# Scores and values of an attention as 64x64 tiles, causal values by key quarters, value banks copied by two engines

## The chip, the cores and the metric

The kernel runs on one core of a Trainium2 chip. Its engines are PE (TensorE, matmuls), ACT (ScalarE), DVE (VectorE), POOL (GpSimd) and SP (SyncE, which issues DMAs). The metric is the device time of one execution in microseconds, as the median of several runs.

## The reference

The input x is (8, 256, 128), in float32. Four blocks are added to it in turn, each on a layer norm of x:

```python
# 1: attention a, 16 heads of 64, over 256 tokens, with a relative bias
scores = einsum('bhid,bhjd->bhij', q, k) * 64**-0.5 + bias
out = einsum('bhij,bhjd->bhid', softmax(scores), v) ... @ w_out.T
# 2: a mixture of 8 experts: router, LN, W1 (128x512), relu, W2 (512x128), times the gate
# 3: attention b, keys and values from a latent (128), causal
att = where(causal, q @ k * 64**-0.5, -inf); y = softmax(att) @ v ... @ w_out
# 4: the same mixture of experts again
```

The function says T = 32 for attention b in its setup, but it takes its length from x, which is 256. In attention a channels of w_qkv are laid out as (d, c, h): the head is the fastest index.

## The kernel before, in words

Each engine has a program of its own, written by hand as a list of steps s. Semaphores tie them: `x.wait_ge(sem, n)` waits, `.then_inc(sem, 1)` signals. The first stage (st = 0) is attention a and its experts, the second (st = 1, causal) attention b and its experts. A stage of attention has 8 batches of 8 units, NU = 64. A unit u is a pair of heads over 256 queries and 256 keys.

One unit goes through these steps. `QK(u)` projects queries and keys of the unit into the bank PT_ (L572), six matmuls in fp32r of high and low parts, and ACT copies them to `qk` (`T`, L918): head 0 lies on partitions 0 to 63, head 1 on 64 to 127. DVE adds the bias or the mask, takes the minimum and writes the scores to `ring` (L1252). ACT takes the exponential in place and the row sum (`expo`, L954), DVE the reciprocal (L1263), POOL weighs the row (L362). `TR(u)` transposes the weighted scores on PE into the banks PP, head 0 in ps4 and head 1 in ps5 (L615, L630); ACT copies the first to `pt` (L932) and DVE the second (L1272). `PV(u)` multiplies by the values: 128 rows (keys) by 64 columns (one head), into one bank PO = ps6, a unit on a half of it (L634). After two units `keep` evicts PO: ACT rounds the bank to `oh` (L908), DVE takes the rest to `ol` (L1222). After eight units `out(b)` projects (L658).

Value matmuls (`values`, L556) make four banks of 128 tokens by 512 channels in a batch, and ACT copies each to `a_v` (L924); spare banks go around among ps1, ps2, ps3 and ps7, which S uses too (`spare`, `claim`).

The order on PE in a step is: QK(s), value matmuls, small pieces, TR(s-4), out. In odd steps S(s-1), S(s), PV(s-5), PV(s-4) follow (L826 to L831). So there is one run of S and PV for each two steps, which is called a step pair. ACT in an even step: keep, T, values, TR, exponentials. DVE in an even step: keep, pieces of the layer norms, TR; in an odd one: TR, S, S.

## Time and profile before

| what | value |
|---|---|
| median of 3 runs | 664.43 us (663.93 to 664.85) |
| span of the profiled execution | 662.1 us |
| median less span | 2.3 us |
| PE, PEld busy | 644.1, 543.7 us |
| DVE, ACT, POOL busy | 475.5, 533.7, 354.5 us |
| granted TensorE clock | 1.00 |

The median is that of the runs; the span is from the first to the last instruction of the one profiled execution. Busy is the time in which at least one instruction of the engine runs; matmuls overlap, so PE is busy also where its pace could be higher. PEld is the loading of weights, which runs beside the matmuls.

### The profile page before, as it was taken

The page shows a single profiled execution, that of the slowest core. Times are in us where ns is not written, and L with a number is a line of the kernel's source. Part 1 is how long each engine was busy: PE and PEld are TensorE (multiplying, and loading weights), DVE is VectorE, ACT ScalarE, POOL GpSimd, SP SyncE. Part 2 cuts the span into 40 slices and gives each one's busy share as a digit, 9 for nine tenths or more (in the row PEclk, how much of TensorE's full clock was granted, in tenths as well). Part 3 has the DMA queues.
Part 4 walks back from the last instruction along what each step waited for, and adds up shares of the span by engine and source line. Part 5 has one row for each costly group of instructions (what it writes and reads, how often), then busy time and mean ns, then how long its engine had stood idle before and what let it go on. Part 6 is the DMA issues. An engine that isn't in the chain of part 4 may idle for free. (4 is left out here: it accounts for less than half of the span.)

```text
span 662.1 us, 17840 instructions
## 1 busy us (share of the span) xinstructions
PE 644.1 (97%) x5406; PEld 543.7 (82%) x5406; DVE 475.5 (72%) x2147; ACT 533.7 (81%) x1776; POOL 354.5 (54%) x669
## 2 busy tenths in 40 slices
PE   5999999999999999999999999999999999999997
PEld 4778887888888788879997788888888888888997
DVE  4866767777786767988755667687768777898834
ACT  3997888889787978785765989898989898986664
POOL 4654545575546644732116545464757575572746
PEclk9999999999999999999999999999999999999999
DMA  9999999999992000035421000000000000003140
GB/s 262 292 296 290 286 230 313 298 272 280 289 286 87 25 1 2 33 98 163 131 65 41 21 1 1 3 1 9 17 15 9 14 25 2 2 34 101 52 132 16
DMA packets 86844, 74.48 MB, mean 112 GB/s; under 512 B 8001, under 2 KB 83399, under 8 KB 86496
## 3 DMA queue, kind: packets, MB, share of 16 engines
q1 hardware_dynamic: 82288, 66.24, 36.5%
q0 software_dynamic: 2848, 6.33, 3.0%
q10 hardware_dynamic: 1616, 0.79, 0.5%
q8 instruction: 45, 0.74, 0.5%
q14 instruction: 47, 0.39, 0.2%
HBM read 19.93 MB, written 54.00 MB: 112 GB/s over the span
## 5 line engine op out<-in xcount | busy, mean ns | idle before, releaser
L362 POOL TENSOR_SCALAR ring<-ring,rs 128x256 f32<-128x256 f32 (+1 forms) x500 | 218.7, 456 | 204.9 <-DVE rs L1263 204.0
L954 ACT ACTIVATE ring<-ring,mn 128x256 f32<-128x256 f32 (+1 forms) x512 | 243.2, 487 | 1.5 <-DVE mn L1252 1.5
L500 PE MATMUL ps<-ident,ring 128*128 128x128 f32 x896 | 120.8, 274 | 1.3 <-POOL ring L362 0.7
L611 PE MATMUL ps<-qk 64*128 64x256 f32 (+1 forms) x1024 | 115.2, 363 | 0.9 <-DVE mn L1252 0.7
L648 PE MATMUL ps<-pt,v 128*64 128x256 f32 (+1 forms) x1024 | 111.4, 359 | 0.2
L500 PEld LDWEIGHTS ps<-ident,ring 128*128 128x128 f32 x896 | 102.1, 143 | 7.6 <-POOL ring L362 2.1
L954 ACT ACTIVATION_READ_ACCUMULATOR ring<-ring,mn 128x1 f32 x512 | 103.6, 202 | 0.0
L648 PEld LDWEIGHTS ps<-pt,v 128*64 128x64 f32 x1024 | 65.5, 136 | 44.4 <-issue 13.3
L611 PEld LDWEIGHTS ps<-qk 64*128 64x128 f32 x1024 | 82.6, 186 | 18.8 <-issue 9.9
L922 ACT COPY qk<-ps 128x512 f32<-128x512 f32 x128 | 74.9, 585 | 23.6 <-PE ps L497 21.9
L1252 DVE CUSTOM_DVE_ANT_0 ring<-ps,cm 128x128 f32<-128x128 f32 (+1 forms) x256 | 73.8, 351 | 1.5 <-issue 1.2
L1281 DVE COPY pt<-ps 128x512 f32<-128x512 f32 x64 | 44.1, 690 | 35.6 <-PE ps L500 35.6
L495 PE MATMUL ps<-xth,wqkh 128*128 128x256 f32 x192 | 64.6, 336 | 0.0
L1003 ACT ACTIVATE f_ht<-ps,f_w 128x128 f32<-128x128 f32 x136 | 38.6, 378 | 21.7 <-PE ps L753 21.7
L1252 DVE CUSTOM_DVE_ANT_0 ring<-ps,T 128x256 f32<-128x256 f32 x136 | 55.5, 417 | 0.0
L497 PE MATMUL ps<-xtl,wqkh 128*128 128x256 f32 x192 | 53.8, 280 | 0.0
L496 PE MATMUL ps<-xth,wqkl 128*128 128x256 f32 x192 | 53.6, 279 | 0.0
L769 PE MATMUL ps<-w,f_ht 128*128 (+1 forms) x400 | 52.4, 277 | 0.4 <-ACT f_ht L1003 0.4
L876 ACT ACTIVATE oh<-ps 128x512 fp32r<-128x512 f32 x64 | 38.3, 598 | 16.7 <-PE ps L648 16.6
L495 PEld LDWEIGHTS ps<-xth,wqkh 128*128 128x128 f32 x192 | 36.0, 188 | 18.6 <-issue 17.4
L1252 DVE CUSTOM_DVE_ANT_1 ring<-ps,T 128x256 f32<-128x256 f32 x120 | 50.0, 417 | 0.2 <-PE ps L611 0.2
L769 PEld LDWEIGHTS ps<-w,f_ht 128*128 128x128 f32 x400 | 48.1, 192 | 1.7 <-issue 1.5
(212 smaller groups left out, 1334.4 us busy)
## 6 DMA issues: line engine op xcount, KB each, us to landing
xs_scratch<-f_ys SPq DMA_DIRECT2D x16, 2064.0 KB, 22.4
yr_scratch<-f_ys SPq DMA_DIRECT2D x8, 1024.0 KB, 10.8
f_xs<-xs_scratch SPq DMA_DIRECT2D x50, 129.0 KB, 2.4
w<-in_W SPq DMA_DIRECT2D x16, 256.0 KB, 6.0
xs_scratch<-f_ys SPq DMA_DIRECT2D x2, 1677.0 KB, 21.8
yr_scratch<-f_ys SPq DMA_DIRECT2D x25, 64.0 KB, 1.6
T<-in_bias SPq DMA_DIRECT2D x2, 512.0 KB, 8.1
T<-in_bias SPq DMA_DIRECT2D x1, 1024.0 KB, 11.0
```

Source lines behind the costliest of these rows:

```text
L362: i = pool.tensor_scalar(ring[:, hh, it, 0:w], ring[:, hh, it, 0:w], rs[:, q], 1.0, ALU.mult, ALU.mult)
L495: pe.matmul(out, ah, bh, start=first, stop=False)
L496: pe.matmul(out, al, bh, start=False, stop=False)
L497: return pe.matmul(out, ah, bl, start=False, stop=last)
L500: return pe.transpose(out, src, ident[:, :])
L611: i = pe.matmul(PS[u % 2][hh][:, 256 * it:256 * it + w], qk[rows, 128 * it:128 * it + 128], qk[rows, 256:256 + w], start=True, stop=True)
L648: i = pe.matmul(PO[64 * hh:64 * hh + 64, col + lo:col + 256], a_v[b % 2][:, jt, 128 * c + 64 * hh:128 * c + 64 * hh + 64], a_pt[(U0 + u) % ...
L769: i = pe.matmul(y_bank(n)[:, 0:128], f_ht[n % 3][:, 128 * f:128 * f + 128], w2[:, bass.ds(e * 4 + f, 1), :].rearrange("p a n -> p (a n)"), ...
L922: act.copy(a_qk[(U0 + u) % 2][:, :], PT_[:, :]).then_inc(a_t, 1)
L954: i = act.activation(ring[:, hh, it, 0:w], ring[:, hh, it, 0:w], ACT.Exp, bias=mn[:, q], scale=-1.0, accum_out=sm[:, q])
L1252: i = dve.tensor_tensor_reduce(ring[:, hh, it, 0:w], bank[:, 256 * it:256 * it + w], table(st, 2 * c + hh, it), 1.0, BIG, ALU.add, ALU.min ...
L1281: i = dve.tensor_copy(pt[:, 1, :], PP[1][:, :])
```

## The change

The ring holds a unit's weighted scores by 64 keys and head, `[it, quarter, head, 64]`, so that one 128x128 transpose gives 64 keys of head 0 on rows 0 to 63 and the same keys of head 1 on rows 64 to 127. S is made by four 64x64 tiles, PV by four 64x64 tiles for each quarter of the keys; PV is called for two units at once, and writes two banks, ps6 (head 0) and ps5 (head 1), which is also the bank of the second half of the transposes. In the causal stage quarter q takes queries from 64q on. Values lie head by row half, so that of each value bank ACT copies 64 partitions and DVE the other 64, to the other half. The order of the heads changes with it (`head_of`, `by_parity`), and the weights of attention b are loaded in ten DMAs with this order in place of two. The bank of the first expert tile's Y becomes ps4.

```diff
-    PO = ps[6]
+    PO = ps[6], ps[5]
-    a_ring = [sb(f"ring{i}", [128, 2, 2, 256], scope=base) for i in range(4)]
+    a_ring = [sb(f"ring{i}", [128, 2, 4, 2, 64], scope=base) for i in range(4)]
-    a_v = [sb("v0", [128, 2, 1024], scope=base)]
+    a_v = [sb("v0", [128, 4, 512], scope=base)]
...
+    def scores(ring, hh, it, w):
+        return ring[:, it, 0:w // 64, hh, :]
+    def by_64(a):
+        return a.rearrange("p (q d) -> p q d", d=64)
+    def head_of(u, hh):
+        return u // 2 * 4 + 2 * hh + u % 2
...
     # PE, S(u)
-                for hh in range(2):
-                    rows = slice(64 * hh, 64 * hh + 64)
-                    i = pe.matmul(PS[u % 2][hh][:, 256 * it:256 * it + w], qk[rows, 128 * it:128 * it + 128],
+                for half_, hh in ((0, 0), (1, 1), (1, 0), (0, 1)):
+                    rows, cols = slice(64 * hh, 64 * hh + 64), slice(64 * half_, 64 * half_ + 64)
+                    i = pe.matmul(PS[u % 2][hh][cols, 256 * it:256 * it + w],
+                                  qk[rows, 128 * it + 64 * half_:128 * it + 64 * half_ + 64],
                                   qk[rows, 256:256 + w], start=True, stop=True)
     # PE, TR(u)
-            for hh in range(2):
-                bank = PP[hh]
+            for jt in range(2):
                 if U0 + u:
-                    pe.wait_ge(v_pt1 if hh else a_pt0, U0 + u)
-                for jt in range(2):
+                    pe.wait_ge(v_pt1 if jt else a_pt0, U0 + u)
+                if U0 + u and jt and u % 2 == 0:
+                    pe.wait_ge(v_o, (U0 + u) // 2)
+                for q in (2 * jt, 2 * jt + 1):
                     for it in range(2):
                         if causal and jt > it:
                             continue
-                        i = tr(bank[:, 256 * jt + 128 * it:256 * jt + 128 * it + 128],
-                               ring[:, hh, it, 128 * jt:128 * jt + 128])
+                        i = tr(PP[jt][:, 256 * (q % 2) + 128 * it:256 * (q % 2) + 128 * it + 128],
+                               ring[:, it, q, :, :].rearrange("p h d -> p (h d)"))
     # PE, PV(u), now for u and u + 1
-            pe.wait_ge(a_pt0, U0 + u + 1)
-            pe.wait_ge(v_pt1, U0 + u + 1)
+            pe.wait_ge(a_pt0, U0 + u + 2)
+            pe.wait_ge(v_pt1, U0 + u + 2)
...
-            for jt in range(2):
-                lo = 128 if causal and jt == 1 else 0
-                for hh in range(2):
-                    i = pe.matmul(PO[64 * hh:64 * hh + 64, col + lo:col + 256],
-                                  a_v[b % 2][:, jt, 128 * c + 64 * hh:128 * c + 64 * hh + 64],
-                                  a_pt[(U0 + u) % 2][:, hh, 256 * jt + lo:256 * jt + 256], start=(jt == 0), stop=(jt == 1))
-            i.then_inc(t_pv, 1)
+            for q in range(4):
+                lo = 64 * q if causal else 0
+                for k, hh in ((0, 0), (1, 1), (0, 1), (1, 0)):
+                    rows = slice(64 * hh, 64 * hh + 64)
+                    i = pe.matmul(PO[hh][64 * k:64 * k + 64, lo:256],
+                                  a_v[b % 2][rows, q, 64 * (c + k):64 * (c + k) + 64],
+                                  a_pt[(U0 + u + k) % 2][rows, q // 2, 256 * (q % 2) + lo:256 * (q % 2) + 256],
+                                  start=(q == 0), stop=(q == 3))
+            i.then_inc(t_pv, 2)
...
     # ACT: keep, values, TR
-            act_high(a_oh[:, c:c + 2, :].rearrange("p c n -> p (c n)"), PO[:, :], a_o)
+            for hh, bank in enumerate(PO):
+                i = act.activation(a_oh[:, c + hh, :], bank[:, 0:256], ACT.Copy, scale=1.0)
+            i.then_inc(a_o, 1)
-            act.copy(a_v[b % 2][:, j, r], ps[bank_of[("v", st, b, n)]][:, :]).then_inc(a_vs, 1)
+            rows = slice(64 * half_, 64 * half_ + 64)
+            act.copy(a_v[b % 2][rows, 2 * j + half_, :], ps[bank_of[("v", st, b, n)]][rows, :]).then_inc(a_vs, 1)
-            if causal:
-                act.copy(pt[:, 0, 0:256], PP[0][:, 0:256])
-                i = act.copy(pt[:, 0, 384:512], PP[0][:, 384:512])
-            else:
-                i = act.copy(pt[:, 0, :], PP[0][:, :])
-            i.then_inc(a_pt0, 1)
+            act.copy(pt[:, 0, :], PP[0][:, :]).then_inc(a_pt0, 1)
     # DVE: values (new, in a step after keep and pre_b, pre_c), keep, TR
+            dve.tensor_copy(a_v[b % 2][64 * half_:64 * half_ + 64, 2 * j + 1 - half_, :],
+                            ps[bank_of[("v", st, b, n)]][64 - 64 * half_:128 - 64 * half_, :]).then_inc(v_vs, 1)
-            low(a_ol[:, c:c + 2, :].rearrange("p c n -> p (c n)"), PO[:, :],
-                a_oh[:, c:c + 2, :].rearrange("p c n -> p (c n)"), a_o, (U0 + u + 2) // 2, v_o)
+            dve.wait_ge(a_o, (U0 + u + 2) // 2)
+            for hh, bank in enumerate(PO):
+                i = dve.tensor_tensor(a_ol[:, c + hh, :], bank[:, 0:256], a_oh[:, c + hh, :].bitcast(F32), ALU.subtract)
+            i.then_inc(v_o, 1)
-            if causal:
-                dve.tensor_copy(pt[:, 1, 0:256], PP[1][:, 0:256])
-                i = dve.tensor_copy(pt[:, 1, 384:512], PP[1][:, 384:512])
-            else:
-                i = dve.tensor_copy(pt[:, 1, :], PP[1][:, :])
-            i.then_inc(v_pt1, 1)
+            late = slice(128 if causal else 0, 256)
+            dve.tensor_copy(*(a.rearrange("p (q i) -> p q i", q=2)[:, :, late] for a in (pt[:, 1, :], PP[1][:, :]))
+                            ).then_inc(v_pt1, 1)
     # PE, step
             if s % 2 and 5 <= s < NU + 4:
                 PV(s - 5)
-                PV(s - 4)
...
```

## Rows read from the trace of the kernel before

**Rows 1.** The page: busy us, share of the span, instructions.
```profile
PE 644.1 (97%) x5406; PEld 543.7 (82%) x5406; DVE 475.5 (72%) x2147; ACT 533.7 (81%) x1776; POOL 354.5 (54%) x669
```

**Rows 2.** Busy time by stretch, first and causal stage; columns named in its head.
```profile
core 0: us, PE busy (x) PEld busy (x) DVE busy (x) ACT busy (x) POOL busy (x), PEclk, DMA share, GB/s
140.00:180.00 40.00, 40.00 (x328) 32.51 (x328) 28.25 (x118) 34.42 (x109) 24.40 (x46) 1.00 1.06 281
180.00:220.00 40.00, 40.00 (x326) 32.92 (x323) 29.68 (x132) 33.46 (x103) 23.17 (x44) 1.00 0.59 172
500.00:540.00 40.00, 39.88 (x358) 33.18 (x356) 30.52 (x165) 35.90 (x134) 27.18 (x54) 1.00 0.05 17
```

**Rows 3.** Timeline, PE, a first-stage pair: start us, duration us, engine, line.
```profile
185.22 2.00 PE L611 MATMUL ps<-qk 64*128 64x256 f32 x16
...
187.15 1.95 PE L648 MATMUL ps<-pt,v 128*64 128x256 f32 x16
...
187.63 1.47 PE L648 MATMUL ps<-pt,v 128*64 128x256 f32 x12
189.02 0.39 PE L495 MATMUL ps<-xth,wqkh 128*128 128x256 f32 x1
189.25 0.28 PE L496 MATMUL ps<-xth,wqkl 128*128 128x256 f32 x1
189.36 0.28 PE L497 MATMUL ps<-xtl,wqkh 128*128 128x256 f32 x1
...
190.89 1.07 PE L500 MATMUL ps<-ident,ring 128*128 128x128 f32 x8
```

**Rows 4.** Timeline, PE, a causal pair.
```profile
530.15 1.58 PE L611 MATMUL ps<-qk 64*128 64x128 f32 x16
531.66 1.52 PE L648 MATMUL ps<-pt,v 128*64 128x256 f32 x16
533.11 0.38 PE L495 MATMUL ps<-xth,wqkh 128*128 128x256 f32 x1
```

**Rows 5.** Timeline, ACT, around the same two pairs.
```profile
186.37 0.57 ACT L941 COPY pt<-ps 128x512 f32<-128x512 f32 x1
...
531.44 0.30 ACT L939 COPY pt<-ps 128x128 f32<-128x128 f32 x1
...
533.36 0.61 ACT L876 ACTIVATE oh<-ps 128x512 fp32r<-128x512 f32 x1
534.13 0.59 ACT L922 COPY qk<-ps 128x512 f32<-128x512 f32 x1 [0.15 <-PE ps L497]
...
535.55 0.37 ACT L938 COPY pt<-ps 128x256 f32<-128x256 f32 x1
```

**Rows 6.** Timeline, DVE, keep and the next copies, with PE's transposes of 517.
```profile
190.51 0.68 DVE L1131 TENSOR_TENSOR ol<-ps,oh 128x512 fp32r<-128x512 f32 x1
192.00 0.69 DVE L1281 COPY pt<-ps 128x512 f32<-128x512 f32 x1 [0.81 <-PE ps L500]
...
517.20 0.82 PE L500 MATMUL ps<-ident,ring 128*128 128x128 f32 x6
...
517.34 0.65 DVE L1131 TENSOR_TENSOR ol<-ps,oh 128x512 fp32r<-128x512 f32 x1
...
535.88 0.42 DVE L1278 COPY pt<-ps 128x256 f32<-128x256 f32 x1 [1.18 <-PE ps L500]
536.22 0.28 DVE L1279 COPY pt<-ps 128x128 f32<-128x128 f32 x1
```

**Rows 7.** DMA issues (KB, us to landing), and the chain of waits: an expert tile.
```profile
bq<-in_w_q SPq DMA_DIRECT2D x1, 512.0 KB, 3.6
...
643.94 0.89 PE ps L769 x8
```

**Rows 8.** Waits: engine and line waiting, releaser, us in total, times, longest.
```profile
PEld ps L648 <- ACT pt L941: 7.2, 21, 0.5
```

**Rows 9.** Groups of ACT, 380 to 620 us: count, busy us, mean ns.
```profile
L876 ACT ACTIVATE oh<-ps 128x512 fp32r<-128x512 f32 x30 | 17.9, 598 | 2.4 <-PE ps L648 2.4
...
L876 ACT ACTIVATE xth<-ps 128x256 fp32r<-128x256 f32 x6 | 2.3, 390 | 0.0
```

More of the change, by code:

```diff
@@ L361, in weigh @@
                     q = slice(2 * hh + it, 2 * hh + it + 1)
-                    i = pool.tensor_scalar(ring[:, hh, it, 0:w], ring[:, hh, it, 0:w], rs[:, q], 1.0,
-                                           ALU.mult, ALU.mult)
+                    part = scores(ring, hh, it, w)
+                    i = pool.tensor_scalar(part, part, rs[:, q], 1.0, ALU.mult, ALU.mult)
             i.then_inc(p_nrm, 1)
@@ L953, in expo @@
                     q = slice(2 * hh + it, 2 * hh + it + 1)
-                    i = act.activation(ring[:, hh, it, 0:w], ring[:, hh, it, 0:w], ACT.Exp,
+                    part = scores(ring, hh, it, w)
+                    i = act.activation(part, part, ACT.Exp,
                                        bias=mn[:, q], scale=-1.0, accum_out=sm[:, q])
@@ L1252, in S @@
                     i = dve.tensor_tensor_reduce(
-                        ring[:, hh, it, 0:w], bank[:, 256 * it:256 * it + w], table(st, 2 * c + hh, it), 1.0, BIG,
+                        scores(ring, hh, it, w), by_64(bank[:, 256 * it:256 * it + w]),
+                        table(st, head_of(c, hh), it), 1.0, BIG,
                         ALU.add, ALU.min, mn[:, 2 * hh + it:2 * hh + it + 1])
@@ L1483, in step @@
                 pre_c(b)
+            for v in VALUES[st].get(s, ()):
+                values(*v)
             if (b := at(s, 13)) is not None and b < NB - 1:
```

92 lines of the change are left out of this document (58 added, 34 removed).

## Prediction

> **What bounds the kernel now.** I read the busy shares first, then the table of stretches, then the timeline of one step pair in each attention stage, engine by engine, then who waits. PE is busy 97% of the span [rows 1]. The stretches show PE at 40.00 and 39.88 of 40 us in the first (bias) and the second (causal) stage, at full granted clock: nothing holds PE there for long. ACT stands at 33.5 of 40 us in the first stage and at 35.9 in the causal one, DVE near 30 in both [rows 2]. So a shorter PE stream shortens the kernel only as far as ACT, first of all in the causal stage, can follow.
>
> The unit of the sum is a step pair: two head pairs, and one run of S(s-1), S(s), PV(s-5), PV(s-4). There are 32 pairs in each stage. A batch has four pairs, and one of them holds the output projection as well, so that it is some 3 us longer on PE.
>
> The first-stage pair in numbers [rows 3]: S starts at 185.22, PV at 187.15, the next QK at 189.02. Its 16 PV matmuls are 8 passes of two tiles side by side. The first two passes take 187.63 - 187.15 = 0.48, the other six and the way out 189.02 - 187.63 = 1.39. With a pass of 0.215 that leaves 0.05 at the entry and 0.10 at the exit. QK's first matmul is followed by the second after 0.23, and by the third after 0.11: an entry of 0.11 with 128 columns of weights. I read each change between tile shapes as an exit of 0.10 plus a first weight load that nothing hides (0.11 for 128 columns, 0.05 for 64). A pair pays three: transposes to S, S to PV, PV to QK.
>
> A rule of the Trainium skill says the same in general: a change of tiling mode drains TensorE, a change of tile within a mode does not (TensorEngine Tiling, Key Properties). The 0.10 exits of rows 3 agree; that 64x64 scores followed by 64x64 values pay none is what the rule adds, as the old kernel never does that.
>
> **What the change takes off PE.** S to PV no longer changes shape: 0.10 + 0.05 = 0.15 a pair. The change into S now loads 64 columns: 0.11 - 0.05, about 0.05. Together 0.20 x 64 = 12.8 us. The matmuls double in number but four run side by side, with the same columns: S costs what it did. In the causal stage the four quarters move 256 + 192 + 128 + 64 = 640 columns where two units with halves move 2 x (256 + 128) = 768, each in two passes. From the two stages' S blocks [rows 3, 4], 1.93 and 1.51 with four passes 128 columns shorter, 128 columns are worth 0.105; 128 columns less in two passes give 0.21 a pair, 6.7 us. The lower bound: the 64-column quarter may go no faster than a 128-column pass, 0.10 a pair, 3.4 us. Transposes stay at eight and six per unit. Sum off PE: 19.5 us, 16 at the lower bound.
>
> The skill has a rule against the narrow quarter: loading weights takes time by their columns, whatever the rows, and overlaps a running matmul where the row groups differ (TensorE: Matmul & The Clock Gate, LDWEIGHTS and Packing small matmuls). Two 64-column loads in each row half would then set 0.11 a pass; by it the sum is the 16 above, and no row here separates the two.
>
> **What it puts in their way.** (a) PV(s-5) and PV(s-4) are now one block, which wants the probabilities of both units at its first matmul. ACT's copy of the odd unit ends at 531.44 + 0.30 = 531.74, PV started at 531.66 [rows 4, 5]. Until now only the second unit needed it, 0.7 us later. PV could start 0.10 earlier, and the copy, now one of 512, ends some 0.03 later, with about 0.05 for the signal: a wait of 0.26. That alone would be small, but ACT in the causal stage has a closed loop: PV's end, keep, the QK copy (534.13, some 0.95 after PV's end at 533.18), values, the copy of the even unit, exponentials, the copy of the odd unit, next PV. ACT also gets work: keep in two pieces (a 256-wide eviction has 0.39 against 0.60 for 512 [rows 9], and two overlap at their ends; about +0.07 a pair), and one 512 copy for 256 + 128 (+0.04 a unit). In the three pairs of a batch without projection ACT then holds the period near where it is: they gain none of their 0.41 (24 x 0.41 = 9.8 us given back), and lose 0.12 a batch, 1.0 us. The eight pairs with projection keep theirs. In the first stage the copy ends at 186.37 + 0.57 = 186.94, 0.21 before PV [rows 3, 5]; less 0.10, and less the signal, the wait is 0.05 to 0.10: 24 x 0.08 = 1.9 us. The 7.2 us noted for this copy are idle weight loads, 21 times 0.34, the entries to PV [rows 8].
>
> (b) The second half of the transposes of an even unit writes the bank that PV's second head has just filled, so it waits for keep, on ACT and then on DVE. PE's cover is QK, the value matmuls and four transposes. Where DVE is free: ol from 190.51 to 191.19, second half at 190.89 + 0.44 = 191.33 [rows 3, 6], 0.14 in hand and about 0.13 more work in keep: no wait. Where DVE is late: ol 517.34 to 517.99, second half at 517.20 + 0.44 = 517.64, 0.35 short [rows 6], near 0.5 with the two pieces. In the first stage one pair of four is of that kind (0.33, 2.6 us). In the causal stage the pairs held by ACT have that time in hand; every other projection pair has not, 0.25 on average, 2.0 us. Queued behind the waiting transpose are QK of the next step and everything after it.
>
> (c) DVE copies half of every value bank: 64 copies of 512, 0.69 each by the pt copy of rows 6, some 0.65 start to start, 42 us of DVE in all; in the causal stage its pt copy falls from 256 + 128 columns to 256, 0.28 less a unit [rows 6]. ACT's value copies stay as long (same width, half the partitions). The new copy falls between keep and the next pt copy, where DVE idles 0.81 and 1.18 [rows 6]. Without that gap (the step with the routing work, one pair in eight) it pushes the odd copy to PV: 3 to 4 pairs of the first stage x 0.65, 2.0 us.
>
> (d) At no price: the three-level access patterns of the ring on POOL, ACT and DVE (bounds: 0, and 5% of their instructions, which on ACT in the causal stage would be 0.18 a pair, 6 us); ten weight DMAs for two, in 256-byte pieces: 3.6 us to landing now [rows 7]; ACT wants them eleven expert tiles of 1.8 us later, two such blocks of 0.89 each, so four times as long would still be hidden. The value banks now wait for two copies before S claims them, with over 1 us in hand.
>
> **The sum.** 19.5 - 9.8 - 1.0 - 1.9 - 2.6 - 2.0 - 2.0 = 0.2 us gained. The span of 662.1 becomes 661.9; the runs' median lies 2.3 above the span, so 664.2; I give 664.0. A measurement of this kernel tells some 0.2% (1.3 us) from no change.
>
> **Rivals.**
> - The PE gain gets through: ACT is busy only 35.9 of 40 us in the causal stage, so it has 10% to give against the 6% that PE wants. If its idle stretches close up, only the first-stage waits and keep's remain: 19.5 - 1.9 - 2.6 - 2.0 = 13, giving 651. Against it: ACT's idle time lies in the projection pair and in front of the QK copy, where it waits for PE and cannot use it. 0.30.
> - Slower: DVE's value copy delays keep's loop. It decides once DVE's gap between keep and the next copy is under 0.65, as then every step's S rows, exponentials and next keep come later, and PE stands at the second half of the transposes. At 0.25 more in each of the 64 pairs, 16 us less 4 that overlap the waits above: 676. For it: the gap in the first stage is only 0.81; against: 10 of 40 us of DVE are idle. 0.19.
> - Four 64x64 tiles do not run side by side but two by two: S and PV double, 3.4 us a first-stage pair and 2.4 a causal one, some 185 us: 850. The old pairs in rows and in columns both overlap, which speaks against. 0.05.
> - The forecast, gains and waits nearly cancel: 0.46, own range 660 to 668.
> The Trainium skill warns of the same end in general: tiling speeds TensorE and not the eviction of PSUM (TensorEngine Tiling, PSUM Bottleneck); rows 2 and 5 are what bears on it here.
>
> **Chances.** Faster: 0.30 and a quarter of the forecast's 0.46, 0.41. Same: 0.20. Slower: 0.39. The range of 8 in 10 goes from 651 (the first rival's time) to 677.
>
> **What would show it.** The changed kernel's timeline should have S and PV one block with no gap of 0.3 in the first stage, about 3.6 us from the first S to QK. In the causal stage PEld of PV should show an idle time of 0.2 to 0.5 on ACT's or DVE's pt copy in three pairs of four, ACT near 37 of 40 us. The transposes should wait for ol in about one pair of four. Wrong would be: a causal pair without projection shorter by 0.3 (ACT was no bound), PE idle before transposes in every pair (DVE is), or S blocks of 3 us (no quads).

## The result, and the profile after

The changed kernel takes 676.53 us (median of 4 runs, 675.63 to 677.88), the kernel before beside it 664.18 (4 runs, 662.89 to 664.85): ratio 1.0181, 95% interval 1.0166 to 1.0195. It is 12.3 us slower; the forecast was no change, 664.0, with a range of 651 to 677 that just holds the measured time. The profiled execution's span is 675.3 us, 13.2 longer than before's 662.1.

The busy line of the page, and the stretches of [rows 2]:

```profile
PE 638.6 (95%) x7454; PEld 536.5 (79%) x7454; DVE 513.2 (76%) x2211; ACT 544.5 (81%) x1776; POOL 353.8 (52%) x669
```

```profile
core 0: us, PE busy (x) PEld busy (x) DVE busy (x) ACT busy (x) POOL busy (x), PEclk, DMA share, GB/s
180.00:220.00 40.00, 39.85 (x480) 31.47 (x483) 33.89 (x143) 34.42 (x113) 21.41 (x41) 1.00 0.49 143
500.00:540.00 40.00, 37.97 (x504) 32.01 (x504) 32.87 (x163) 36.21 (x123) 24.63 (x49) 1.00 0.04 11
```

PE is no longer always busy in the causal stage (37.97 of 40 for 39.88 [rows 2]), and DVE has 4.2 and 2.4 us more in the same 40. PE has less work to do, and waits more. The timeline of PE in a first-stage pair, against [rows 3]:

```profile
188.21 1.04 PE L530 MATMUL ps<-ident,ring 128*128 128x128 f32 x8
189.18 1.96 PE L643 MATMUL ps<-qk 64*64 64x256 f32 x32
190.96 1.95 PE L686 MATMUL ps<-pt,v 64*64 64x256 f32 x32
192.84 0.38 PE L525 MATMUL ps<-xth,wqkh 128*128 128x256 f32 x1
...
194.72 1.27 PE L530 MATMUL ps<-ident,ring 128*128 128x128 f32 x8
```

From the first S to QK it is 192.84 - 189.18 = 3.66 for 189.02 - 185.22 = 3.80 [rows 3]. But the eight transposes behind take 1.27 for 1.07: their second half stands for keep. In the table of waits (engine and line, releaser, us in total, times, longest) two are new, and one has doubled against [rows 8]:

```profile
PE ps L530 <- DVE ol L1270: 9.5, 18, 1.3
...
PEld ps L686 <- ACT pt L977: 15.5, 31, 1.0
PE ps L686 <- ACT pt L977: 4.7, 12, 0.8
```

For the accounting I cut the executions at the first PV of step pairs 0, 1, 28, 31 (the last of the first stage), 32, 60 and 63. The table gives these stretches for each kernel's profiled execution, in us; "whole" is the ratio of its runs' time to that of the kernel before beside it. (The last stretch is taken from the span in tenths, and so is good to 0.05.)

```
kernel               to     1 to 28  28 to 31  31 to 32  32 to 60  60 to 63  63 to  span   whole
                     pair 0 1st st.  its end   experts   causal    its end   end
before               29.48  239.91   23.21     69.18     216.35    21.10     54.87  662.1  1
changed              32.89  240.94   25.29     70.75     219.33    22.29     55.98  675.3  1.0181
s_quads_alone        29.20  238.80   23.22     69.50     215.36    21.31     54.79  660.2  0.9977
old_split_values     32.98  242.58   23.19     69.43     223.40    21.25     56.21  676.9  1.0195
old_pv_both          29.96  240.12   23.28     68.76     221.22    21.27     54.69  667.3  1.0079
old_tr_keep          29.12  241.61   24.15     68.93     221.60    21.21     55.76  670.4  1.0155
old_all_waits        31.57  242.14   23.78     69.75     223.36    21.45     54.33  674.4  1.0165
start_act            33.30  240.83   25.29     69.83     219.37    22.28     55.41  674.3  1.0178
keep_split           32.73  239.42   24.63     69.80     219.02    21.64     55.07  670.4  1.0134
copy_early           31.62  247.47   26.06     70.24     227.50    23.02     56.01  690.5  1.0458
values_act           33.03  245.00   25.30     71.65     226.27    22.29     54.56  686.3  1.0371
key_halves           31.43  240.84   25.30     70.49     223.12    22.27     54.64  676.2  1.0227
causal_values_dve    31.14  240.86   25.29     71.04     224.60    23.58     54.36  679.0  1.0262
dve_copies_cut       32.85  239.32   25.30     70.05     217.50    22.30     55.96  671.4  1.0132
act_copies_cut       31.96  240.97   25.31     70.26     219.54    23.55     55.07  674.8  1.0173
dve_copies_late      32.74  245.05   25.30     70.20     220.81    23.28     55.42  680.9  1.0258
values_by_dma       194.07  239.30   25.30     84.16     217.54    23.57     54.61  846.5  1.2771
dma_and_keep_split  195.47  236.68   24.62     81.88     215.79    21.63     54.71  838.6  1.2703
tile_before_copy     32.47  239.48   24.64     69.83     217.35    21.64     54.86  668.2  1.0103
tile_and_dve_cut     32.70  236.73   24.64     70.54     214.26    21.63     55.42  663.9  1.0008
```

The 13.2 us (the stretch between pairs 0 and 1, not shown, gives 0.2 back): start 3.4, first stage 1.0, its end 2.1, experts 1.6, causal stage 3.0, its end 1.2, the rest 1.1. The stretch 31 to 32 holds the last first-stage pair, the experts and the opening of the causal stage. The expert stretches vary by 0.7 or more between executions with the same code there, and so does the start: 31.14 to 32.89 in six forms whose start is the changed kernel's, 29.12 to 31.57 in four whose start is that of before (the last section says by what). The attention stretches repeat within 0.2, and comparisons below go by them. Where a text below says in front of what PE stands longer, it compares the start-to-start distances of PE's matmuls one by one, which can be done where two kernels issue the same list.

### The profile page after: what moved, and what is told of

Its sections match the earlier page's. It is cut to its first block and busy times, and to the rows that moved or that the text cites. A ratio compares the mean times of both kernels' runs of the same rounds, so it can differ in the third digit from the quotient of the medians.

```text
span 675.3 us, 22111 instructions
## 1 busy us (share of the span) xinstructions
PE 638.6 (95%) x7454; PEld 536.5 (79%) x7454; DVE 513.2 (76%) x2211; ACT 544.5 (81%) x1776; POOL 353.8 (52%) x669
## 5 line engine op out<-in xcount | busy, mean ns | idle before, releaser
L530 PE MATMUL ps<-ident,ring 128*128 128x128 f32 x896 | 127.0, 277 | 10.0 <-DVE ol L1270 9.5
L643 PE MATMUL ps<-qk 64*64 64x256 f32 (+1 forms) x2048 | 112.4, 356 | 1.3 <-DVE mn L1298 0.7
L686 PE MATMUL ps<-pt,v 64*64 64x256 f32 (+3 forms) x2048 | 103.1, 339 | 5.1 <-ACT pt L977 4.7
L686 PEld LDWEIGHTS ps<-pt,v 64*64 64x64 f32 x2048 | 73.9, 133 | 35.9 <-ACT pt L977 15.5
L990 ACT ACTIVATION_READ_ACCUMULATOR ring<-ring,mn 128x1 f32 x512 | 99.8, 195 | 0.0
L1325 DVE COPY pt<-ps 128x512 f32<-128x512 f32 (+1 forms) x128 | 71.3, 557 | 36.1 <-PE ps L530 34.3
L643 PEld LDWEIGHTS ps<-qk 64*64 64x64 f32 x2048 | 65.8, 132 | 29.9 <-issue 12.3
L977 ACT COPY pt<-ps 128x512 f32<-128x512 f32 x128 | 74.0, 578 | 4.6 <-PE ps L530 4.2
L955 ACT ACTIVATE oh<-ps 128x256 fp32r<-128x256 f32 x128 | 41.5, 377 | 14.7 <-PE ps L686 14.0
L1270 DVE TENSOR_TENSOR ol<-ps,oh 128x256 fp32r<-128x256 f32 x128 | 47.3, 409 | 4.7 <-ACT oh L955 4.5
```

The costliest lines, as they stand in the source:

```text
L530: return pe.transpose(out, src, ident[:, :])
L643: i = pe.matmul(PS[u % 2][hh][cols, 256 * it:256 * it + w], qk[rows, 128 * it + 64 * half_:128 * it + 64 * half_ + 64], qk[rows, 256:256 + ...
L686: i = pe.matmul(PO[hh][64 * k:64 * k + 64, lo:256], a_v[b % 2][rows, q, 64 * (c + k):64 * (c + k) + 64], a_pt[(U0 + u + k) % 2][rows, q // ...
L977: act.copy(pt[:, 0, :], PP[0][:, :]).then_inc(a_pt0, 1)
L990: i = act.activation(part, part, ACT.Exp, bias=mn[:, q], scale=-1.0, accum_out=sm[:, q])
L1325: dve.tensor_copy(*(a.rearrange("p (q i) -> p q i", q=2)[:, :, late] for a in (pt[:, 1, :], PP[1][:, :]))).then_inc(v_pt1, 1)
```

## The experiments

**One part of the change in the kernel before.** s_quads_alone has only the scores as 64x64 tiles (the S edit of the diff).

> The kernel before, with its scores alone made by four 64x64 tiles; transposes, probabilities times values, keep and all copies as before. The changed kernel's block of S is 0.04 shorter (1.58 for 1.62 in the first stage, 1.16 for 1.20 in the causal one), and the way from the transposes into S is 0.20 in both. If the four tiles are worth that wherever PE never stands, 64 x 0.04 = 2.6 us come off: 660.5. Rival: in the causal stage ACT's loop gives the pace already in the kernel before, and 32 x 0.04 = 1.3 us come off: 662. If the shorter S is owed to the fact that the following PV has the same shape, nothing comes off: 663.

Measured 662.72 us (12 runs), ratio 0.9977 (0.9968 to 0.9987): a little faster, and by that the fastest of all forms here. Both stages give 1.1 and 1.0 over 28 pairs, 0.04 each: S is 1.58 for 1.62 and 1.16 for 1.20. The stretches speak for the first theory: PE gave the pace in both stages of the kernel before, the causal one too. The ratio (1.5 us, 0.9 to 2.1) is nearer to the rival's total; what the attention stages give, the rest does not quite pass on.

old_split_values divides only the copies:

```diff
-            act.copy(a_v[b % 2][:, j, r], ps[bank][:, :]).then_inc(a_vs, 1)
+            act.copy(a_v[b % 2][0:64, j, r], ps[bank][0:64, :]).then_inc(a_vs, 1)
+    # DVE, where the changed kernel has it
+            dve.tensor_copy(a_v[b % 2][64:128, j, r], ps[bank][64:128, :]).then_inc(v_vs, 1)
```

> The kernel before, with only the copies of the value banks divided: ACT takes partitions 0 to 63 of each bank, DVE 64 to 127 (64 copies of some 0.65 more on DVE; ACT's keep their length). Theory that these copies cost much of the 12 us: the start loses the 2.1 to 2.4 us that all forms of the changed kernel lose there beside the clock, and each batch loses where DVE's gap is under 0.65, 0.2 to 0.3 a batch in both stages, 4 us more: 669. Rival, the term of the prediction: 2.0 us in all, 665 to 665.5. Third: DVE's idle time hides all but the start: 665.4, the start's lag in the trace tells it from the second.

Measured 677.47 us, ratio 1.0195 (1.0177 to 1.0213): 13 us, as much as the change loses in all, and more than any of the theories gave. ACT gets nothing back, as the two groups of copies in the changed kernel show (last but one number: mean ns of one; the third part: idle before), and below them one copy of the kernel before (start, duration):

```profile
L1263 DVE COPY v<-ps 64x512 f32<-64x512 f32 x64 | 43.9, 688 | 3.4 <-PE ps L527 0.2 <-DVE run L1227 0.2
...
L970 ACT COPY v<-ps 64x512 f32<-64x512 f32 x64 | 37.1, 580 | 7.5 <-PE ps L527 1.1
```

```profile
527.77 0.59 ACT L930 COPY v<-ps 128x512 f32<-128x512 f32 x1
```

Half the partitions, the same time: ACT's copy of 64 partitions takes 580 ns where that of 128 took 0.57 to 0.59 us. The start takes 3.5, the 28 causal pairs 7.1, those of the first stage 2.7 (the profiled execution is 14.8 longer than that of the kernel before; 1.3 of it lie in the last stretch, which scatters). In the pairs the time is lost at two places, as the waits of this kernel show:

```profile
PE ps L502 <- DVE ph L1155: 5.3, 13, 0.7
PE ps L502 <- DVE pt L1291: 2.0, 6, 0.5
```

`ph` are the layer-normed rows for the router, a piece that DVE makes once a batch; PE transposes them behind QK. In the kernel before PE waits for them once, 0.2 us. DVE's list has the value copy directly in front of this piece (DVE's timeline: the end of keep, value copy, `ph`, pt copy without a stop), so that `ph` comes later by a copy, some 0.65:

```profile
441.59 0.66 DVE L1135 TENSOR_TENSOR ol<-ps,oh 128x512 fp32r<-128x512 f32 x1
442.28 0.69 DVE L1232 COPY v<-ps 64x512 f32<-64x512 f32 x1
443.00 0.71 DVE L1155 TENSOR_SCALAR ph<-row,m,r 128x128 f32<-128x128 f32 x2
443.75 0.42 DVE L1290 COPY pt<-ps 128x256 f32<-128x256 f32 x1
```

In front of the transposes of `ph` PE stands 2.2 us longer in the first stage and 4.2 in the causal one, and 2.9 in the causal stage's transposes of the scores, which wait for DVE's pt copy, the next thing in DVE's list. The start, PE's timeline first in this kernel and then in the changed one:

```profile
24.24 0.44 PE L502 MATMUL ps<-ident,xh 128*128 128x128 f32 x2 [0.50 <-DVE mn L1264]
25.02 0.63 PE L502 MATMUL ps<-ident,won 128*128 128x128 f32 x4 [0.34 <-DVE mn L1264]
26.43 0.63 PE L502 MATMUL ps<-ident,won 128*128 128x128 f32 x4 [0.78 <-DVE v L1232]
```

```profile
24.32 0.44 PE L530 MATMUL ps<-ident,xh 128*128 128x128 f32 x2 [0.51 <-DVE mn L1298]
25.10 0.63 PE L530 MATMUL ps<-ident,won 128*128 128x128 f32 x4 [0.34 <-DVE mn L1298]
26.49 0.63 PE L530 MATMUL ps<-ident,won 128*128 128x128 f32 x4 [0.77 <-DVE v L1263]
```

The same three gaps; in the kernel before PE has none of them. In batch 0 of the changed kernel DVE has no idle time (3.97 of 4.00 us busy at 20 to 24), two value copies at 19.90 push back the S rows and the normed rows (xh), and two more at 25.66 hold the banks into which the output weights are transposed.

start_act lets ACT copy both halves in batch 0:

```diff
+            if B0 + b == 0:
+                act.copy(a_v[0][other half of rows, 2 * j + 1 - half_, :], ps[bank][other half, :])
             act.copy(a_v[b % 2][rows, 2 * j + half_, :], ...).then_inc(a_vs, 1)
```

> In batch 0 of the first stage alone, ACT copies both halves of every value bank (eight copies) and DVE none; all else is the changed kernel. Theory: DVE's value copies of batch 0 stand ahead of the layer norm pieces and of the claims that PE waits for, and PE's gaps at 19 to 27 us (0.51, 0.34, 0.77) also bring the half clock of 27 to 30 us; without them the kernel gains 3.0 to 3.5 us over the changed one: 673.3, 9 slower than before. Rival (the time is lost in each pair, and the start only moves it): the start gets shorter by the 1.6 us of the three gaps or less, 675. If ACT is what is full at the start, its four more copies of 0.6 cost what they save: 676.5.

Measured 675.46 us, ratio 1.0178 (1.0158 to 1.0197): no gain, pair 0 at 33.30. ACT is as full there (3.96 of 4.00 us at 20 to 24), and PE stands 0.45 for a value copy and 0.91 for ACT's pt copy instead. The last answer of the expectation comes nearest: the copies cost about the same, whoever makes them. The trace of this start is not clean: it keeps the full clock, but has the slow early stretch of the last section.

**The waits of the change, in the kernel before.** old_pv_both:

```diff
-            pe.wait_ge(a_pt0, U0 + u + 1)
-            pe.wait_ge(v_pt1, U0 + u + 1)
+            pe.wait_ge(a_pt0, U0 + (u | 1) + 1)
+            pe.wait_ge(v_pt1, U0 + (u | 1) + 1)
```

> The kernel before, but PV of the even unit waits for the copies of both units' probabilities, as in the changed kernel. In the causal stage ACT's copy of the odd unit ends some 0.13 behind PV's start (signal included), in the first stage 0.2 ahead of it. Theory of the prediction, ACT's loop: 0.13 in each causal pair without projection, and as PV's end, keep and the next QK copy follow, nothing makes up for it: 24 x 0.13 = 3 us, 667. Rival: PE catches up what it waits, as ACT is idle for 4 of 40 us: under 1 us, 664.

Measured 668.96 us, ratio 1.0079 (1.0061 to 1.0097): 4.9 us in the causal pairs, 0.2 in the first stage. The theory's place is right, its size is low (0.17 a pair).

old_tr_keep:

```diff
                     pe.wait_ge(v_pt1 if hh else a_pt0, U0 + u)
+                if U0 + u and hh and u % 2 == 0 and u < NU - 4:
+                    pe.wait_ge(v_o, (U0 + u) // 2)
```

> The kernel before, with one wait more: the transposes of an even unit's second head wait for keep's last eviction, as they must in the changed kernel (not those of the last four units of a stage). Theory: 0.3 where DVE is late, one pair of four in the first stage and every second in the causal one, 8 x 0.3 + 16 x 0.3 = 7 us: 670 to 671. Rival: keep in one piece is out in time and DVE's free time covers it (the wait is 0.14 ahead in the pair shown): 2 us at most, 665 to 666.

Measured 673.76 us (672.04 to 677.91), ratio 1.0155 (1.013 to 1.018): 8.3 us by the spans (670.4; the execution with the profile is the fastest of six, and the medians are 9.8 apart), with 1.7 in the first stage, 0.9 at its end, 5.3 in the causal one.

old_all_waits is both, and keep in two pieces of 256 columns.

> Both waits together in the kernel before, and keep in two pieces of 256 columns on ACT and on DVE. If each counts by itself the sum is 3 + 4 to 7 + some 0.1 in each of 64 pairs (the pieces): 673 to 678, the waits of the changed kernel without its gain on PE and without DVE's value copies. Rival: they fall on the same loop and the largest counts: 668 to 670. If the total is under 667, the changed kernel's causal pairs are held by something none of these contains.

Measured 675.22 us, ratio 1.0165 (1.0142 to 1.0189), but in the 28 causal pairs 7.0 us where the two alone made 4.9 and 5.3, and 2.2 in the first stage. They do not add up; that they share one loop is the likely reading, not shown by a run of its own.

**The waits in the changed kernel.** keep_split evicts ps5 first and signals it apart (on ACT likewise):

```diff
-            for hh, bank in enumerate(PO): ... ol ...
-            i.then_inc(v_o, 1)
+            for hh, ready, done in ((1, a_o1, v_o1), (0, a_o, v_o)):
+                dve.wait_ge(ready, (U0 + u + 2) // 2)
+                dve.tensor_tensor(ol of hh ...).then_inc(done, 1)
     # PE, TR: the second half waits for v_o1
```

> Keep evicts ps5 first, on ACT and on DVE, with a semaphore of its own, and the second half of the transposes waits for that bank only. Theory that the wait of the transposes for keep costs on the path: their waits for ol (9.5 us in all, 18 waits of 0.5) shorten by the time of one eviction on each engine, 0.3 to 0.4, and some two thirds of it get through: 4 to 6 us faster than the changed kernel, 671 to 672. Rival (in the causal stage ACT's loop holds the period, and in the first stage DVE's): the waits vanish from the list and come back in front of PV: under 1.5 us, 675 to 676.5.

Measured 672.25 us, ratio 1.0134 (1.0116 to 1.0151), 3 to 4 us less. It comes from the first stage (1.5) and the two ends (0.7 each), where no QK stands between PV and the transposes. There the changed kernel waits longest (timeline, PE):

```profile
293.68 0.63 PE L530 MATMUL ps<-ident,ring 128*128 128x128 f32 x4 [1.27 <-DVE ol L1270]
```

In the causal pairs it is only 0.3. The transposes give 4.0 back there, but PE stands 2.0 longer in front of `ph` and 1.4 in front of PV. The wait for `ph`, in the changed kernel and in this one:

```profile
PE ps L530 <- DVE ph L1187: 2.0, 7, 0.3
```

```profile
PE ps L531 <- DVE ph L1187: 4.8, 12, 0.6
```

So the theory is right in the first stage and at the ends. In the causal stage the rival is right that the waits come back, but most of it comes back at `ph` and not at PV.

copy_early makes ACT's copy of the odd unit ahead of head 1's exponentials:

```diff
                 after(s)
+                if s >= 5:
+                    TR(s - 4)
                 expo(s - 3, (1,))
```

> In an odd step ACT copies the odd unit's transposed rows (pt) before the exponentials of the second head instead of behind them. Theory that PV waits for ACT's copy because of where it stands in ACT's list: the 15.5 + 4.7 us noted for PV's first weights and matmuls on ACT's pt fall to under 6, and the causal stage gains 0.1 to 0.2 a pair, 3 to 6 us in all: 671 to 673. Rival (ACT is full, and what is moved forward pushes back the exponentials, the next T and the next copies): within 1 us of the changed kernel, 675.5 to 677.5.

Measured 693.72 us, ratio 1.0458 (1.044 to 1.0477): neither. PV's wait is gone (0.20 from S to PV in nearly all pairs), and this stands in its place:

```profile
PE ps L530 <- DVE ol L1272: 27.1, 34, 1.7
```

The exponentials now stand between the copy and keep, so keep starts 2.54 us behind the copy for 1.66 (median of the causal pairs), and PE waits for it in the transposes. ACT's order is squeezed between two deadlines, PV and keep.

**The copies in the changed kernel.** values_act gives all to ACT, two of 64 partitions each.

> ACT copies both halves of every value bank, in two instructions of 64 partitions; DVE copies none (64 copies of 0.65 to 0.69 leave DVE, 64 of 0.55 to 0.6 come to ACT). Theory that DVE's value copies are what costs (they stand between keep, the S rows and the next pt copy): the first stage gains 3 us at its start and up to 4 behind it, and the causal stage loses at most 2: 671 to 673. Rival that ACT is the bound in the causal stage: 32 copies of 0.6 lie on its loop there, 19 us, of which ACT's idle time (3.8 of 40 us) absorbs a half: 684 to 690. Both can hold, each in its stage; the lag at the end of the first stage against the changed kernel tells the first, the causal stage the second.

Measured 687.69 us, ratio 1.0371 (1.0351 to 1.0392): 6.9 more in the causal pairs (ACT is busy 38.03 of 40 us, and PE stands 5.8 longer in front of PV and 3.7 in front of the transposes), and the first stage loses 4.1 as well, where a gain was expected. The wait for `ph` is gone (2.7 us in the causal pairs), and outweighed. causal_values_dve gives DVE both halves in the causal stage.

> The changed kernel, with both halves of each value bank copied by DVE in the causal stage (32 copies of 0.55 leave ACT there, 32 of 0.65 come to DVE); the first stage as it is. Theory that ACT's loop (PV, keep, QK copy, value copy, copy of the even unit, exponentials, copy of the odd unit) sets the causal pace in the pairs without projection: each pair with values gets up to 0.55 shorter until PE or DVE is the bound; PE alone has 0.3 to 0.4 a pair to give, so 5 to 8 us: 669 to 671. Rival: DVE (32.9 of 40 us) is as near its own loop, and its keep and pt copies come later by 0.65: the gain is eaten up, 676 to 679.

Measured 681.32 us, ratio 1.0262 (1.0244 to 1.0279): 5.3 us slower in the causal pairs: 2.4 more in front of `ph`, 3.4 in the transposes. The rival's case, and dearer than it said. In dve_copies_late only DVE's order changes (copies behind its pt copy of the step).

> The changed kernel, with DVE's value copies (all but those of the very first batch) behind its pt copy in the step and no longer before it. Theory that their place is what costs, since the pt copy that PV waits for, or the keep wait, comes 0.65 later for them: half or more of the 8 us of the cut go, 670 to 672. Rival: DVE has no room for 0.65 at all in these steps, the S rows behind them come later instead, and with them the exponentials: 675 to 678.

Measured 681.02 us, ratio 1.0258 (1.0244 to 1.0273): slower in both stages, by 4.1 and 1.5. The wait for `ph` is gone here too (1.4 and 2.7 us), but PE stands 3.4 and 1.9 longer in front of S, and 2.4 and 1.3 in front of PV. Of these two places for the copies the old one is the better; a third, behind `ph` and ahead of the pt copy, was not tried. dve_copies_cut and act_copies_cut take the copies out of one queue:

```diff
+            w = 512 if b < 2 else 8
```

> The changed kernel, but from batch 2 of each stage on DVE copies 8 of a value bank's 512 columns only (the same 64 instructions and signals; the other columns keep old values, that much of the result is left out). In the kernel before with only the copies divided, the time went up by 13.3 us, 3.5 of them at the start, 2.5 in batches 1 to 7 of the first stage, 7 in the causal one. Theory that DVE's copies are what turned the change's gain into a loss: six of eight batches lose them here, 2.1 + 5.5 us and a little: 667 to 669. Rival (ACT's order and keep's wait are the bound in the changed kernel, and DVE's copies only fill what would be idle): 673 to 676.

Measured 672.58 us, ratio 1.0132 (1.0116 to 1.0148): 1.6 and 1.8 us in the two stages, where all eight batches' copies had cost the old kernel 2.7 and 7.1 (in proportion to the pairs concerned, an estimate, 2.0 and 5.3). It is just under the range of the rival, and far from the theory: in this kernel the copies fill in part what would be idle. What goes is the wait for `ph`, 1.4 and 2.7; other waits take back 0.9 in the causal stage.

> The changed kernel, but from batch 2 of each stage on ACT copies 8 of each value bank's 512 columns (the other columns keep old values, that much of the result is left out); DVE's copies stay whole. ACT loses some 0.45 in each pair. If ACT's loop holds the causal pairs without projection (PV waits for ACT's pt copy 0.1 to 0.6 there), they get 0.1 to 0.35 shorter until PE holds them: 18 x 0.25 = 4 to 5 us in the causal stage, 1 in the first: 670 to 671. Rival: DVE's copies and the wait for keep hold them, and ACT's idle time only grows: 675 to 676.5.

Measured 676.00 us, ratio 1.0173 (1.0156 to 1.019): nothing in the 28 pairs of either stage. The theory falls: ACT's queue as a whole does not hold the pairs. ACT's timeline of a causal pair of the changed kernel shows why (the read-outs of the row sums are left out):

```profile
511.55 0.64 ACT L955 ACTIVATE oh<-ps 128x256 fp32r<-128x256 f32 x2
...
512.97 0.58 ACT L970 COPY v<-ps 64x512 f32<-64x512 f32 x1
...
513.80 0.59 ACT L977 COPY pt<-ps 128x512 f32<-128x512 f32 x1 [0.25 <-PE ps L530]
...
514.28 0.40 ACT L990 ACTIVATE ring<-ring,mn 128x128 f32<-128x128 f32 x1
...
515.17 0.57 ACT L962 COPY qk<-ps 128x512 f32<-128x512 f32 x1
...
516.65 0.57 ACT L977 COPY pt<-ps 128x512 f32<-128x512 f32 x1
```

```profile
517.27 0.45 PE L686 MATMUL ps<-pt,v 64*64 64x256 f32 x4 [0.27 <-ACT pt L977]
```

Behind the value copy ACT stands 0.25 for PE's transposes; from there its list (copy, two tiles, QK copy, a small piece of the routing, two tiles, copy) runs without a stop for 517.22 - 513.80 = 3.42 us, and PV starts 0.05 later. The loop is PE from PV to the first transposes, then ACT for 3.42. A shorter value copy only lengthens the 0.25, as the same copy of pt in act_copies_cut shows:

```profile
512.87 0.59 ACT L978 COPY pt<-ps 128x512 f32<-128x512 f32 x1 [0.67 <-PE ps L530]
```

tile_before_copy (on keep_split) puts the first 128-wide exponential tile of an even step ahead of the copy, into that idle time:

```diff
+            early = causal and s % 2 == 0 and 8 <= s < NU
+            if early:
+                expo(s - 2, (0,), (0,))
             if 4 <= s < NU + 4:
                 TR(s - 4)
```

> The kernel with keep's banks apart (keep_split), and in the even steps of the causal stage ACT takes the exponential of the first tile (128 wide, 0.39) ahead of the copy of the even unit's pt, where it stands idle for PE's transposes (0.25 in the pair read), and no longer behind it. Theory of a loop through PE (PV, QK, values, first transposes) and ACT (copy of the even unit, two tiles, QK copy, two tiles, copy of the odd unit; 3.4 us): ACT's part of it gets 0.39 shorter, PE's part up to 0.14 longer, 0.25 a pair where PV waits for the copy (18 of 28 pairs), 4 us: the 28 causal pairs take 215 in place of 219.0, the whole 668.5. Rival: ACT's work as a whole, or DVE's, holds the pairs: nothing moves, 672 to 672.5.

Measured 671.10 us, ratio 1.0103 (1.0077 to 1.0129): the causal pairs take 217.35 for 219.02, 1.7 us of the 4 expected. ACT's run is 3.01 now:

```profile
509.64 0.57 ACT L977 COPY pt<-ps 128x512 f32<-128x512 f32 x1
...
512.08 0.57 ACT L977 COPY pt<-ps 128x512 f32<-128x512 f32 x1
```

PE stands 4.3 us less in front of PV in the 28 pairs, so the place is right. But 2.8 of them come back one step on, in front of the odd unit's transposes: these wait for the even unit's copy, which the tile has pushed back.

```profile
PE ps L531 <- ACT pt L977: 1.2, 5, 0.3
```

> The same, and DVE copies 8 of 512 columns of each value bank from batch 2 of each stage on (that much of the result is left out). With DVE's copies gone from the kernel with keep's banks apart, the 28 pairs took 236.7 in the first stage and 215.8 in the causal one (the run with DMAs). If the loop through PE and ACT is what is left of the causal stage, its 28 pairs take 212 to 213, and the whole is 661 to 663, the first form of the changed kernel to be faster than the kernel before in spite of the start. Rival: 215.5 again, 664.5 to 665.5.

Measured 664.61 us (12 runs), ratio 1.0008 (0.9993 to 1.0022): the causal pairs take 214.26 us, between the two. The loop is real (1.5 to 1.7 us each time), and is not all that holds the stage. With keep apart, DVE's copies are worth 3.1 in the causal stage and 2.7 in the first, more than without it (1.8 and 1.6): the wait for `ph` that keep_split had made longer is gone, 4.2 us in the causal pairs. Even so the kernel is no faster than the one before.

**The quarters.** key_halves:

```diff
-                lo = 64 * q if causal else 0
+                lo = 128 * (q // 2) if causal else 0
```

> The changed kernel, with causal values by halves of the keys in place of quarters: quarter q takes queries from 128 x (q // 2) on, so that PV moves 768 columns in two passes in place of 640 (what is added are zeros). If PE gives the pace of the causal stage, PV gets 0.21 longer in 32 pairs, 6.7 us: 683. If ACT's loop gives it, as the prediction had it, PV's length counts in that loop too (keep waits for PV's end), and the full 0.21 comes back: 683 as well. Rival: the narrow quarters run at the pace of the loading of their weights, and 0.10 a pair is all they save: 679.5. Third: DVE's keep and copies hold the causal stage and leave PE waiting for other reasons: under 2 us, 678.

Measured 679.25 us, ratio 1.0227 (1.0211 to 1.0243). PV is 1.21 to 1.26 and its exit 0.20, for 1.05 to 1.10 and 0.15: the 0.21 of the prediction is there on PE. But only 3.8 us of 5.9 come out over 28 pairs (0.135 a pair): PE stands 1.3 longer in front of PV, and 3.1 less in the transposes, where it had waited before. So the rival's total was right, and its reason was not.

**Values by DMA.** ACT copies the bank whole into a free buffer, SP moves the halves:

```diff
+                for r in (1 - half_, half_):
+                    sp.dma_start(a_v[b % 2][to, 2 * j + r, :], f_xt[k % 2][64 * r:64 * r + 64, :]).then_inc(d_v[k % 2], 16)
```

> The changed kernel, but ACT copies each value bank whole (128 partitions x 512, one instruction as in the kernel before) into one of two buffers in SBUF that the attention stages do not use, and two DMAs of 64 partitions, issued by SP, bring its halves to their rows; DVE copies nothing. If DVE's copies are what cost, and the DMAs arrive before PV (a step and a half later, against 2 to 3 us for a DMA): 13 us less than the changed kernel at most, 664 to 666, the start included. Rival: the DMAs of the fourth bank of a batch come too late for PV, 1 us in each of 16 batches: 680. Or the keep wait and ACT's loop take over what DVE gives: 668 to 671.

> Values by DMA as in the kernel beside it, and keep evicting ps5 first with a semaphore of its own. The two are independent if the one took time in DVE's queue and the other at the transposes: 4.3 us less than with the DMAs alone, 659 to 662, faster than the kernel before. Rival: once DVE has no value copies, keep's second eviction comes early enough anyway, and the split gives under 1.5 us in place of 4.3.

Measured 848.11 and 842.85 us, ratios 1.2771 and 1.2703. No theory had this: ACT waits 164.7 us for the first value DMAs. SP issues them behind the filling of the scratch tensors in memory and the experts' weights (waits of values_by_dma, and three of its groups of DMAs with KB each and us to landing):

```profile
ACT f_xt L970 <- DMA v<-f_xt: 177.0, 3, 164.7
```

```profile
xs_scratch<-f_ys SPq DMA_DIRECT2D x16, 2064.0 KB, 19.5
...
yr_scratch<-f_ys SPq DMA_DIRECT2D x8, 1024.0 KB, 10.0
...
w<-in_W SPq DMA_DIRECT2D x16, 256.0 KB, 6.0
```

The filling is the greater part by far: these 24 issues move 41 MB, the weights 4 MB. Behind that the stages run as with dve_copies_cut (239.30, 217.54), a second witness of what DVE's copies cost in these pairs; keep_split on top gives 2.6 and 1.75. A kernel with these DMAs on another queue was not tried.

## Why the prediction was wrong

The sum had next to nothing net in the two stages: 6.4 us of gain against 6.5 of waits in the first, 13.1 against 12.8 in the causal one. It had no term for the start or the openings of the stages, and for the ends only what the waits cost in an ordinary pair. Of the 13.2 us by which the span grew, the 28-pair stretches of the two stages hold 4.0, the start 3.4, the two ends 3.3, the stretch from 31 to 32 1.6 and the rest 1.1, less 0.2. So the greater part of the miss lies where the sum had nothing, and 3.0 in the causal pairs.

- **What comes off PE: right.** Per first-stage pair S is 0.04 shorter, the gap from S to PV 0.20 for 0.31, PV 0.04 shorter: 0.19 for 0.20. Per causal pair S is 0.05 shorter, the gap 0.11, PV 0.20 (1.05 for 1.25; 1.10 where PV had to wait) and its exit 0.05: 0.41 for 0.41. S still waits 0.20 behind the transposes, so the 0.05 at the entry did not come, and the gap gave 0.11 of its 0.15; the rest came off inside the blocks. In s_quads_alone, where only S has the new shape, the gap stays at 0.31. The rule of the Trainium skill that a change of mode drains and a change of tile does not (TensorEngine Tiling, Key Properties) agrees with that. The Trainium skill's rule on loading weights by columns (TensorE: Matmul & The Clock Gate, LDWEIGHTS), by which the narrow quarter would have saved only half, does not bind here: quarters in place of halves took 0.21 off PV and its exit.
- **DVE's value copies, "2.0": the step that failed.** They cost 13 us in the kernel before. I looked for the gap of 0.81 and 1.18 in the steady pair and took the copy as hidden; I did not price the start, where DVE is full (1.7 to 2.5, and 1.5 more by the clock), nor ask what the 0.65 pushes behind it. It pushes `ph`, for which PE waits once a batch, and the pt copy: 2.7 in the first stage, near my 2.0 but by another wait, and 7.1 in the causal one, where I had nothing. In the changed kernel, where other waits fill the same time, the copies are worth 3.4 in six batches of eight, besides the start. That 13 is also the size of the whole loss is a coincidence: alone in the old kernel the copies cost 13.3 and the waits 11.3 (old_all_waits), 24.6 together, PE's gain is 19.2 over 64 pairs, and the difference is 5.4, not 12.3. The runs show which parts cost, and not a sum of them.
- **The transposes' wait for keep, "-2.6 -2.0": right in place, low.** 8.3 us in the kernel before; 9.5 us of PE waiting in the changed one, 18 waits in 64 pairs, about the one in four of the forecast. The ends of the stages, without QK as cover, were left out: 1.27 for one wait. The two ends are 3.3 us longer, of which keep_split takes back 1.3; at the first one PV also waits once 0.83 for ACT's pt copy.
- **ACT's loop, "-9.8 -1.0 -1.9": right in kind, wrong in content.** The waits for the odd unit's copy are there in 17 of 30 causal pairs (S to PV takes 0.3 to 0.8 in place of 0.20) and in 4 of 30 of the first stage. But the loop does not hold ACT's value copy or its total work; it is 3.42 us of ACT behind PE's transposes in the pair read. The causal stage had 0.41 x 28 = 11.5 us less on PE and took 3.0 more: 14.5 given back, for the 12.8 of the terms in 32 pairs (11.2 in 28).
- **Terms added as if each stood alone.** Measured alone the three causal costs are 4.9, 5.3 and 7.1, and the first two with the pieces 7.0. That my causal terms came within 3.3 us in the pairs is luck: each was priced low, and adding them counted too much.
- **(d), what had no price: right.** ACT's exponentials take 479 ns in the mean for 487, POOL's weighing 452 for 456, DVE's scores 351 and 417 as before, so the ring's access patterns cost nothing. The ten weight DMAs land after 3.8 to 4.5 us (medians of their three groups) for 3.6 before.
- **The rivals.** The one that came out is "slower", 676, by DVE's value copy; its time is right to 1 us, partly by luck. Its mechanism is only partly right: the 0.25 a pair shows in the causal stage of old_split_values, but 0.10 in the first, PE stands in front of `ph` more than in front of the second half of the transposes, and the start was not in it. "Side by side" is settled: no S block of 3 us.
- **Open:** the stretch from 31 to 32 is 1.6 longer and the last one 1.1. The last one is scatter (55.1 in the mean of the six old forms, 55.2 in the twelve changed ones without DMAs). The other is not: 68.76 to 69.75 in the old forms, 69.80 to 71.65 in the changed ones, 1.1 apart in the mean. Half of that lies in the causal stage's opening, from its first S to the last S before pair 32: 13.1 us for 12.5, and 13.0 in old_split_values, so by the value copies again. The rest was not found. The end of the causal stage takes 23.3 to 23.6 in place of 22.3 in four changed forms (act_copies_cut among them); why was not found either. What holds the causal stage behind the loop through ACT and the wait for `ph` was not tried further.

## What to carry to other kernels

Dividing a PSUM copy by partitions between two engines takes nothing off the first and gives the second the whole again: here 64 partitions cost what 128 do. Price an added instruction where its engine is fullest (the start, the ends, the step with side work), not in the steady pair, and ask of everything behind it in the list who waits for it: here it was a small piece made once a batch. When a stage runs at 97% of one engine, several loops stand right behind it: try each new wait alone in the old kernel, and expect neither the costs nor the gains to add up.

## What the hardware showed besides

After the three gaps at the start the granted clock fell to its lower level (1.2 GHz) in the changed kernel, and the same happened in old_split_values, tile_before_copy and tile_and_dve_cut. The stretch of the changed kernel, columns as in [rows 2]:

```profile
27.00:30.50 3.50, 3.50 (x20) 3.50 (x18) 2.05 (x3) 2.61 (x7) 0.17 (x1) 0.51 1.10 317
```

That adds some 1.5 us to its start: key_halves, with the same code and gaps there, kept the full clock and reached pair 0 at 31.43. Nor do the gaps alone decide: PE was busy 2.57 of 4.00 us at 24 to 28 here, and 2.38 in keep_split, which kept 1.00.

A second stretch of the kind lies further ahead, in old and new forms alike. QK's matmuls took 0.41 for 0.28 there, from 10.3 to 14.8 us in old_all_waits:

```profile
9.39 1.12 PE L500 MATMUL ps<-ident,wqn 128*128 128x128 f32 x4 [0.94 <-DMA wkn<-in_w_qkv]
...
11.37 0.41 PE L496 MATMUL ps<-xth,wqkl 128*128 128x256 f32 x1
```

0.41 is also their time under the granted 0.51, but the clock column says 1.00 for this stretch; so it is like the lower level, and not shown to be it. In the six executions where it is long (old_all_waits, start_act, keep_split, values_act, dve_copies_cut, dve_copies_late) the first value matmul starts at 17.02 to 18.00 us, in those without it at 15.36 to 15.93. The wait for the first weights is longer in the six (0.60 to 0.94) than in those without it (0.15 to 0.59). But old_pv_both, act_copies_cut and dma_and_keep_split have a shorter stretch of the kind with waits of 0.32 to 0.53, so what brings it on is not shown. A start can gain or lose 1.5 us from one execution to the next, and no single execution tells that from a change in the code.
